# Raw expert weights loaded two experts ahead into their own f16 bytes, in the first stage of a two-layer kernel on one core

## What is computed

```python
logits = xt @ gate_w.T                                   # xt: 4096 x 256, normalized
_, idx = jax.lax.top_k(logits + beta, K)                 # K = 2 of E = 8 experts
probs = jax.nn.sigmoid(jnp.take_along_axis(logits, idx, axis=-1))
c = jnp.zeros((B, E), xt.dtype).at[jnp.arange(B)[:, None], idx].add(probs)
g = jnp.einsum('bh,ehm->bem', xt, gate_proj_w)           # 8 x 256 x 512
u = jnp.einsum('bh,ehm->bem', xt, up_proj_w)             # 8 x 256 x 512
h = jax.nn.silu(g) * u
eo = jnp.einsum('bem,emh->beh', h, down_proj_w)          # 8 x 512 x 256
combined = jnp.einsum('beh,be->bh', eo, c)
```

## Time and profile before

| | |
|---|---|
| three timed runs | 3520.72, 3512.49, 3509.45 us (median 3512.49) |
| the profiled execution | 3520.69 us, span 3518.9 us |
| PE busy over the span | 3220.9 us (92%) |
| DVE busy | 2810.6 us (80%) |
| ACT busy | 2318.1 us (66%) |
| POOL busy | 1648.7 us (47%) |
| granted clock of PE, mean | 0.960 |
| first stage: first `weight_max` / last `weight_max` starts | 16.2 / 393.4 us |
| first row of the experts stage | 441.3 us |
| ACT, a scaled copy of one matrix (lines 493, 497) | 1.14 us, 48 times |
| ACT, the copy of 128 x 1024 from PSUM (lines 542, 547) | 1.01 us |

### The profile page before, as it was taken

One profiled execution on the slowest core, in us unless ns is written; L12 is line 12 of the kernel. 1 busy time (PEld: TensorE's weight loads), 2 busy tenths in 40 slices (PEclk: granted clock), 3 DMA queues, 4 the chain that ended last, 5 costly groups with the idle time before them and its releaser, 6 DMA issues. The chain is left out here.

```text
span 3518.9 us, 61065 instructions
## 1 busy us (share of the span) xinstructions
PE 3220.9 (92%) x19800; PEld 1295.5 (37%) x19815; DVE 2810.6 (80%) x4905; ACT 2318.1 (66%) x3660; POOL 1648.7 (47%) x2104
## 2 busy tenths in 40 slices
PE   6777789999999999999999999868999999999987
PEld 3434456663222222222222222252333333333333
DVE  5564643468999999999999999476888999889997
ACT  3342333335888888788888878856767767777763
POOL 1331340002444444434344444405777888888885
PEclk9887899998999999999999999988999999999998
DMA  3233221111111111111111111041222222222221
GB/s 126 95 102 97 99 74 55 54 49 44 31 50 39 39 38 36 35 35 35 35 32 34 30 30 31 17 156 52 70 72 65 75 82 70 73 81 69 73 75 52
DMA packets 160888, 211.62 MB, mean 60 GB/s; under 512 B 32324, under 2 KB 108364, under 8 KB 160604
## 3 DMA queue, kind: packets, MB, share of 16 engines
q1 hardware_dynamic: 141340, 172.51, 16.4%
q0 software_dynamic: 8512, 18.76, 1.7%
q10 hardware_dynamic: 10752, 16.78, 1.4%
HBM read 154.48 MB, written 52.69 MB: 59 GB/s over the span
## 5 line engine op out<-in xcount | busy, mean ns | idle before, releaser
L1408 ACT ACTIVATE prob<-psS 128x1024 f32<-128x1024 f32 (+3 forms) x1280 | 1104.4, 906 | 278.9 <-PE psS L1592 269.4
L1458 DVE TENSOR_REDUCE pmax<-psR 128x1 f32<-128x512 f32 x1674 | 1057.0, 684 | 78.4 <-PE psR L1534 46.6
L2234 POOL TENSOR_TENSOR hc<-h_d,crep 128x512 f32<-128x512 f32 x512 | 646.9, 1271 | 189.8 <-DVE h_d L2463 139.6
L1534 PE MATMUL psR<-kslab,qslab 48*128 48x512 bf16 (+3 forms) x2480 | 652.5, 351 | 22.4 <-DVE pmax L1458 14.0
L1607 PE MATMUL psVo<-prob,vaug 128*32 128x512 f32 (+3 forms) x5120 | 629.8, 546 | 1.3 <-ACT ov L1412 0.6
L1592 PE MATMUL psS<-qslab,kslab 51*128 51x512 bf16 (+3 forms) x2560 | 533.3, 354 | 39.9 <-ACT prob L1408 23.0
L2463 DVE TENSOR_TENSOR_SCAN h_d<-a,state,psU 128x512 f32<-128x512 f32 x384 | 489.3, 1275 | 0.0
L1323 POOL TENSOR_SCALAR_AFFINE_SELECT prob<-prob 128x256 f32<-128x256 f32 (+1 forms) x512 | 213.4, 420 | 533.1 <-ACT prob L1408 533.1
L2453 DVE TENSOR_TENSOR psU<-dtx,psX 128x512 f32<-128x512 f32 x512 | 356.2, 696 | 92.7 <-PE psX L2613 42.8
L1534 PEld LDWEIGHTS psR<-kslab,qslab 48*128 48x128 bf16 x2480 | 187.2, 94 | 629.0 <-DVE pmax L1458 478.6
L2366 ACT ACTIVATE a<-dt,a_neg 128x512 f32<-128x512 f32 x512 | 366.9, 724 | 54.1 <-DVE h_d L2463 53.2
(11 more groups left out here) (347 smaller groups left out, 5260.8 us busy)
## 6 DMA issues: line engine op xcount, KB each, us to landing
crep<-c_rows_d SPq DMA_DIRECT2D x256, 256.0 KB, 3.1
x_e<-rows_d SPq DMA_DIRECT2D x72, 128.0 KB, 2.0
y_d<-y SPq DMA_DIRECT2D x72, 128.0 KB, 1.7
q_d<-parts SPq DMA_DIRECT2D x48, 128.0 KB, 2.3
k_d<-parts SPq DMA_DIRECT2D x48, 128.0 KB, 2.3
qslab<-q_d SPq DMA_DIRECT2D x60, 96.0 KB
kslab<-k_d SPq DMA_DIRECT2D x60, 96.0 KB
raw_w<-n_L_ffn_gate_proj_w_dram ACTq DMA_DIRECT2D x8, 512.0 KB, 3.8
```

Source lines behind the costliest of these rows:

```text
L1408: act.activation(prob[g % BUFS][:, :, off:BLK], psS[g % 2][:, :, off:BLK], ACT.Exp).then_inc(prob_ready, 1)
L1458: dve.tensor_reduce(into[:, lo:lo + (count - 1) * NEXT + 1:NEXT], psR[at % BANKS][:, 0:count * w].rearrange("p (n w) -> p n w", w=w), AX.X ...
L1534: ins = pe.matmul(dst[:, m * w:(m + 1) * w], qslab[u][rows, i * P:(i + 1) * P], kslab[u][rows, ch * BLK:ch * BLK + w], start=(m == 0), sto ...
L2234: pool.tensor_tensor(hc[:, g % CR], h[:, g % HR], crep[:, g // PAIR % SPR], ALU.mult).then_inc(hc_ready, 1)
```

## The change

The tile `raw_w` is gone. Each matrix has one tile for both parts, `wg`, `wu`, `wd`, in which an expert's high part (1024 f16) and low part (1024 f16) lie side by side. Read as f32, these are 1024 columns, and the raw matrix of that expert is loaded into them. Every expert so has bytes of its own for its raw weights, and a load waits only for the loads before it. `load_expert(1)` now stands ahead of block 0, and `load_expert(n + 2)` where `load_expert(n + 1)` stood.

Since the high part overwrites half of the raw weights, the scaled weights go first, into a new tile `scaled_w` of the size of the old `raw_w`. ACT writes `scaled_w` from the raw weights, then the high part from `scaled_w` by a plain cast, and POOL the difference. `scaled_weights(e, w)` waits until POOL has taken the difference of the same matrix of expert e - 1. `weight_max` reads three tiles, by three instructions. The experts stage reads the parts at new addresses.

```diff
--- before.py
+++ after.py
@@ -151,8 +151,10 @@
         gate_rows = hT[0:E, 0, 0:D]
         y = sg[:].rearrange("p s (j d) -> p (s j) d", d=D)
         wsg, wsu, wsd = sb("wsg", [P, KD, M]), sb("wsu", [P, KD, M]), sb("wsd", [P, M // P, D])
-        raw = sb("raw_w", [P, 3, KD * M])
-        zeros = raw[:, 0, 0:D]
+        scaled = sb("scaled_w", [P, 3, KD * M])
+        zeros = scaled[:, 0, 0:D]
+        raw = [keep[name][:].rearrange("p e x m -> p (e x m)").bitcast(F32).rearrange("p (e m) -> p e m", e=E)
+               for name in ("wg", "wu", "wd")]
         wmax = sb("wmax", [P, 3])
         wmax_r = sb("wmax_r", [3, 1])
         diag_r = sb("diag_r", [3, 3])
@@ -198,7 +200,7 @@
         raw_in = sem("a_raw_in")
         wscale_step = sem("a_wscale_step")
         wmax_moved = sem("a_wmax_moved")
-        whigh_ready = sem("a_whigh_ready")
+        wsplit_step = sem("a_wsplit_step")
         wlow_ready = sem("a_wlow_ready")
 
         block = ctx.enter_context(nc.Block())
@@ -269,11 +271,10 @@
         def _(pool):
 
             def low_weights(e):
-                for w, low in enumerate((keep["wgl"], keep["wul"], keep["wdl"])):
-                    high = (keep["wgh"], keep["wuh"], keep["wdh"])[w]
-                    pool.wait_ge(whigh_ready, 3 * e + w + 1 + CREDIT)
-                    pool.tensor_tensor(low[:, e].rearrange("p k m -> p (k m)"), raw[:, w],
-                                       high[:, e].rearrange("p k m -> p (k m)"), ALU.subtract).then_inc(wlow_ready, 1)
+                for w, name in enumerate(("wg", "wu", "wd")):
+                    pool.wait_ge(wsplit_step, 6 * e + 2 * w + 2 + CREDIT)
+                    pool.tensor_tensor(keep[name][:, e, 1], scaled[:, w], keep[name][:, e, 0], ALU.subtract)\
+                        .then_inc(wlow_ready, 1)
 
             c = Chain(pool, pchain)
             c.after(pool.memset(keep["ident"][:], 0.0))
@@ -394,7 +395,9 @@
             def weight_max(e):
 
                 dve.wait_ge(raw_in, 48 * e + 48 + CREDIT)
-                dve.tensor_reduce(wmax[:], raw[:], AX.X, ALU.max, apply_absolute_value=True).then_inc(wscale_step, 1)
+                for w in range(3):
+                    ins = dve.tensor_reduce(wmax[:, w:w + 1], raw[w][:, e], AX.X, ALU.max, apply_absolute_value=True)
+                ins.then_inc(wscale_step, 1)
 
             def weight_row(e):
                 dve.wait_ge(wmax_moved, 2 * e + 1 + CREDIT)
@@ -481,20 +484,23 @@
         def _(act):
 
             def load_expert(e):
-                act.wait_ge(wlow_ready, 3 * e + CREDIT)
+                act.wait_ge(raw_in, 48 * e + CREDIT)
                 for w, (name, rows) in enumerate((("gate_proj", KD), ("up_proj", KD), ("down_proj", M // P))):
-                    act.dma_start(raw[:, w].rearrange("p (k m) -> p k m", k=rows),
+                    act.dma_start(raw[w][:, e].rearrange("p (k m) -> p k m", k=rows),
                                   io[name][e].rearrange("(k p) m -> p k m", p=P)).then_inc(raw_in, 16)
 
+            def scaled_weights(e, w):
+
+                act.wait_ge(wscale_step, 3 * e + 3 + CREDIT)
+                if e:
+                    act.wait_ge(wlow_ready, 3 * e - 2 + w + CREDIT)
+                act.activation(scaled[:, w], raw[w][:, e], ACT.Copy, scale=keep["wscale"][:, w, e:e + 1])\
+                   .then_inc(wsplit_step, 1)
+
             def high_weights(e, w):
 
-                act.wait_ge(wscale_step, 3 * e + 3 + CREDIT)
-                high = (keep["wgh"], keep["wuh"], keep["wdh"])[w]
-                act.activation(high[:, e].rearrange("p k m -> p (k m)"), raw[:, w], ACT.Copy,
-                               scale=keep["wscale"][:, w, e:e + 1])
-
-            def scaled_weights(e, w):
-                act.activation(raw[:, w], raw[:, w], ACT.Copy, scale=keep["wscale"][:, w, e:e + 1]).then_inc(whigh_ready, 1)
+                act.wait_ge(wsplit_step, 6 * e + 2 * w + 1 + CREDIT)
+                act.copy(keep[("wg", "wu", "wd")[w]][:, e, 0], scaled[:, w]).then_inc(wsplit_step, 1)
 
             load_expert(0)
             act.wait_ge(gate_t, 1 + CREDIT)
@@ -548,30 +554,31 @@
 
             token_root(0)
             copy_turned(0)
+            load_expert(1)
             for n in range(NBLK):
                 scores(n)
                 copy_rows(n, 0)
                 copy_rows(n, 1)
                 gate(n, 0)
                 gate(n, 1)
-                high_weights(n, 0)
                 scaled_weights(n, 0)
                 if n + 1 < NBLK:
                     token_root(n + 1)
                 copy_rows(n, 2)
+                high_weights(n, 0)
+                scaled_weights(n, 1)
+                copy_rows(n, 3)
+                gate(n, 2)
                 high_weights(n, 1)
-                copy_rows(n, 3)
-                scaled_weights(n, 1)
-                gate(n, 2)
+                scaled_weights(n, 2)
+                gate(n, 3)
                 high_weights(n, 2)
-                gate(n, 3)
-                scaled_weights(n, 2)
                 if n + 1 < NBLK:
                     copy_turned(n + 1)
                 copy_shared(n)
                 copy_values(n)
-                if n + 1 < NBLK:
-                    load_expert(n + 1)
+                if n + 2 < NBLK:
+                    load_expert(n + 2)
             assert E == NBLK
 
         @block.tensor
@@ -1022,8 +1029,8 @@
                         if dst is psU:
                             max_product(i, 0)
                         for k in range(KD):
-                            w_high, w_low = (keep[w + part][:, bass.ds(e, 1), k].rearrange("p o m -> p (o m)")
-                                             for part in "hl")
+                            w_high, w_low = (keep[w][:, bass.ds(e, 1), part, k * M:(k + 1) * M].rearrange("p o m -> p (o m)")
+                                             for part in range(2))
                             ins = split_products(dst[:], xTh[:, s, k], xTl[:, s, k], w_high, w_low, k == 0, k == KD - 1)
                         ins.then_inc(done, 1)
                 max_product(i, 1)
@@ -1033,8 +1040,8 @@
                     if known(i - 1, 1):
                         pe.wait_ge(y_ready, i - 1 + CREDIT)
                     for m in range(MT):
-                        w_high, w_low = (keep["wd" + part][:, bass.ds(e, 1), m].rearrange("p o d -> p (o d)")
-                                         for part in "hl")
+                        w_high, w_low = (keep["wd"][:, bass.ds(e, 1), part, m * D:(m + 1) * D].rearrange("p o d -> p (o d)")
+                                         for part in range(2))
                         ins = split_products(psY[:], hTh[:, 1 - s, m], hTl[:, 1 - s, m], w_high, w_low, m == 0, m == MT - 1)
                     ins.then_inc(d_done, 1)
                 max_product(i, 2)
@@ -2692,10 +2699,8 @@
                 keep["hot"] = sb(moe, "hot_all", [P, NBLK, 2, TPB, E])
                 keep["slot"] = sb(moe, "slot_all", [P, NBLK, 2 * TPB])
                 keep["table"] = sb(moe, "table", [P, 2, RT], I32)
-                for part in "hl":
-                    keep["wg" + part] = sb(moe, "wg" + part, [P, E, KD, M], F16)
-                    keep["wu" + part] = sb(moe, "wu" + part, [P, E, KD, M], F16)
-                    keep["wd" + part] = sb(moe, "wd" + part, [P, E, M // P, D], F16)
+                for name in ("wg", "wu", "wd"):
+                    keep[name] = sb(moe, name, [P, E, 2, KD * M], F16)
                 keep["wmag"] = sb(moe, "wmag", [P, 3, E])
                 keep["wscale"] = sb(moe, "wscale", [P, 3, E])
                 keep["onehot"] = sb(moe, "onehot", [P, E, RT])
```

## The result

| | median (range) of the runs, us | ratio to before, 95% interval |
|---|---|---|
| before | 3516.6 (3509.5 to 3522.0) | |
| after | 3467.94 (3463.66 to 3474.16) | 0.9867 (0.9843 to 0.9892) |

The kernel is 48.7 us faster; the forecast was 3462, with 3448 to 3477 as its range. Further down, one execution of `spread_behind_u0` (7995.74 us) and one of `all_four` (7611.33 us) took more than twice as long as the others; the medians given for these two kernels are over all four executions, the ratios leave the long ones out.

A forecast was written before the change was run, and what follows sets the result against it. It took the first stage's blocks to be bound by a chain passing between engines, with choose waiting for weights. 47.5 + 0.5 + 2.0 = 50 us off the 3512.5 us median gave 3462 us, range 3448 to 3477.

The forecast's parts named there:

- `choose` follows the sigmoid: First stage, seven block boundaries: choose waits for the sigmoid instead of the weights, 6.64 to 6.97 us each, 47.5 us.
- No issue behind block 6: Last boundary of the first stage: no loads issued ahead of the sigmoid's table load, 0.5 us saved once.
- PE not cold at q1: First stage, choose to last hidden tile: PE runs on from q0, 30.15 us in blocks 1 to 6; 2.0 us saved.
- What was costed at nothing: Split reduces (3.4 to 4 us, covered), moved ACT work, block 0's issues, longer register rows in experts stage: 0 us.
- (a) the stall: First stage, DVE's cut: one operation of 7.11 us instead of 0.69, during POOL's three differences, was to stay.
- (b) the wait ahead of the down product: First stage: PE's 6.92 us wait for the last hidden tile, and the product's cold start, were to stay.
- The down product did not change: Rival 1, first stage: down product runs at the upper clock, another 16 us gone, 3447 us; chance 0.07.
- rival 2: First stage: denser transfers or the table load give back 5 us a boundary, 3475 to 3480 us; chance 0.11.
- The Trainium skill's drain: First-stage boundaries: about 1.38 us added per table switch, choose 1.4 us later, seven boundaries giving about 38 us; not taken.
- PE's queue in the experts stage: Rival 3: long register rows slow 288 psY groups, 3534 us at 0.25 us each; chance 0.02 slower, 0.02 nearly all lost.
- the loads did come earlier: Rival 4, first stage: ACT's own wait ahead of the loads holds them, so no earlier in effect, 3510 us; chance 0.02.

The follow-up runs named there:

- spread_behind_u0: Kernel after with PE's spread_max moved behind the product u0 instead of ahead of it; 3415.14 us, ratio 0.9706.
- all_four: Kernel after with spread_max behind u0, early sigmoid table, POOL's differences held back in blocks 0 to 6, loads ahead of both copies; 3390.79 us, ratio 0.9632.
- late_loads: Kernel after with its loads issued one block later again, at the old time, all else as changed; 3518.92 us, ratio 1.0005.
- early_load_old_tile: Kernel before, with its one raw-weight tile, and the next expert's load moved ahead of the down-product and values copies; 3460.98 us, ratio 0.9844.
- sigmoid_table_early: Kernel after plus a one-column sigmoid ahead of copy_shared, so the table is loaded before the logits come; 3452.45 us, ratio 0.9815.
- two kernels with the hold: POOL's differences wait, in blocks 0 to 6, until DVE has made the last hidden tile: in kernel after 3408.21 us, in kernel before 3450.43 us.
- Three edits: Kernel after with spread_max behind u0, early sigmoid table and loads ahead of both copies, POOL's differences not held back; 3455.54 us, ratio 0.9822.
- differences_after_hidden: Kernel after with POOL's three differences held back until DVE has made the last hidden tile, blocks 0 to 6; 3408.21 us, ratio 0.9683.
- all_four_held_in_last_block: Version all_four with POOL's differences held back in block 7 as well; 3387.81 us, ratio 0.9635.

## Why the prediction was right, and where it was not

**`choose` follows the sigmoid, 47.5 us.** Right: 47.91 measured, and `choose` starts 0.09 us behind the end of the scores (164.58 to 164.67). `late_loads` shows that this is the loads' time and nothing else.

**No issue behind block 6, 0.5 us.** Right in size: from the last hidden tile to the experts stage's first row 15.1 us before, 14.7 after.

**PE not cold at q1, 2.0 us.** This term failed. It assumed a stretch of 30.15 us in blocks 1 to 6 (which by its own six numbers gives 2.1, not 2.0) and gave bounds of 0 and 2.5; measured, the six are 30.17, 31.82, 31.81, 30.11, 30.21 and 31.85, and the term is -2.9. I had foreseen that PE would be early and wait for `diag_r`, but at 1.5 us, and at no further price. It is 2.00, because the issues of the loads stand ahead of the sigmoid; and in three blocks of six u0 then runs at the lower level (3.4 to 3.7 us for 1.98). The first cause is shown by `early_load_old_tile`, the price by it and `sigmoid_table_early`: without a slow u0 their six stretches sum to 181.12 and 181.01 us, 2 us below the 183.04 of before, as forecast. The block period came out at 47.1 us, not 46.4.

**The sum.** 50 forecast; the first stage gave 45.2, and the profile's 50.1 reached it only with a shorter state-space stage that isn't the change's. Of the 5.9 us between 3462 and the median, 4.1 are the median of before, 3516.6 in this set where the forecast started from 3512.5.

**What was costed at nothing.** The reduces take 1.21 us each, 3.46 in all, inside 3.4 to 4 and under DVE's pause. ACT's casts take 1.04 us. Three issues in block 0 leave 1.95 us of idle time ahead of its sigmoid. The experts stage lasts 365.5 us before and 366.9 after, but 365.6 in `all_four` with the same layout. Over all profiles it is 365.5 to 366.2 with the old layout and 365.6 to 367.0 with the new: the longer register rows cost about 1 us at most.

**(a) the stall and (b) the wait ahead of the down product stay.** Right for the kernel after (6.95 and 6.92 us). The reason that I gave was POOL's three differences, and two kernels with the hold confirm it. What I did not see is how near the edge it stood. By the earlier trace rows the held operation is the second of the cut's four, and it started at 204.85, 0.26 us ahead of POOL. The fourth would have started 1.19 us behind it and ended at 206.73, and POOL began at 205.11. DVE missed by 1.62 us, and I read the meeting as a fixed property of the block. It was the largest sum in the stage: about 60 us, with or without the change.

**The rivals.** The down product did not change: 8.6 to 10.1 us behind the same wait. Nothing was given back in the boundaries; what was given back, 2.9 us, was given back in the stretches. (The first stage's transfers aren't the densest of the kernel, as rival 2 has it: the page of before has 95 to 126 GB/s there and 156 in a later slice.) The table load costs its 1.28 us and no more: `sigmoid_table_early` took away 1.28 and 0.50. The Trainium skill's drain (ScalarE: Activation LUTs, What ACT_TABLE_LOAD costs), by which I had worked out 38 us as the estimate in place of 47.5, doesn't appear in these rows. PE's queue in the experts stage did not show, and the loads did come earlier.

## What to carry to other kernels

- Where a wait ends late because of a transfer, first ask whether its issue can move, and only then whether it needs memory of its own: two moved lines gave 7 us more than the new layout.
- An operation that lasts ten times its like was here a meeting of two engines, not a property of the operation. Read from the timeline when the last operation that can be held would end, by how much that misses the other engine's start, and price the order in which it would be through in time.
- An edit that wins such a meeting by 0.2 us wins it in one version and loses it in the next. Three edits, of which two had each given time alone, gave 40 us less together than one of them, until a wait fixed the order; and a hold is only worth something where nothing that matters runs under the held work, as the last block showed.

## What the runs showed of the hardware that was not expected

- **DVE and POOL.** While POOL took its three differences back to back, one DVE operation from SBUF to SBUF (a cast or a subtraction of 128 x 512) was held through all three, 6.2 to 7.3 us, in each of the 76 blocks of the 14 profiles in which DVE wasn't through with its cut when POOL began. In 73 of them the held operation had started first, by 0.04 to 0.55 us (POOL's rows are rough); each ended 0.28 to 0.57 us behind the last difference. An operation that had ended 0.12 us ahead of POOL took its usual 0.69 (block 7 of the kernel after). The hidden tile, which reads PSUM, started 0.29 us behind a difference in block 7 of `spread_behind_u0` and took no longer. The reduces of 1024 columns ran beside the differences at their 1.21 us in `all_four`. The Trainium skill (SBUF — State Buffer, Who interferes with whom) has a lock held per instruction, by whoever begins first. The blocks fit neither half of it. Behind the last block of `all_four_held_in_last_block` a DVE operation was let in between two differences, the first after 2.12 us; the same operation, in the same place, took 5.23 us in `spread_behind_u0`, to the end of the third. What makes the difference is open.
- **The clock behind a short wait.** PE's wait of 2.00 us was followed by a u0 at the lower level (1.2 GHz) in 5 of 12 blocks of the two profiles of the kernel after, and in none of the 6 in `differences_after_hidden`, where the down product ahead of it had run at the upper level (2.4 GHz). Behind 1.52 us and 0.88 us it happened in none of the 14 blocks of `early_load_old_tile` and `sigmoid_table_early`. The wait alone doesn't decide it; what PE did before counts. The 12 blocks of the kernel after fall apart cleanly by the length of the down product ahead: the 5 with a slow u0 had one of 9.71 to 10.08 us, the 7 others one of 8.58 to 9.66.
- **A stage that no edit touches.** The state-space stage lasted 1082.1 to 1082.3 us in six profiles, 1086.0 in two and 1089.8 to 1090.6 in six, with the same program. Both profiles of the kernel before are among the longer ones, `late_loads`, no faster than it, and `early_load_old_tile`, with its layout, among the shorter; what sets it wasn't tried.
